# A fused four-layer kernel: 1/smooth moved from the attention outputs (DVE) to per-head copies of the values (GpSimd)

## The reference, cut to what matters

```
q, qx, k, v = fp8 linears of the normalised input     # 16 heads, 8 groups, 128 wide
kx, vx      = linear(context)                         # the "second" keys and values
core = softmax(q k^T / sqrt(128)) v                   # two heads share one k, v
xout = softmax(qx kx^T / sqrt(128)) vx
catq = fp8( clip( concat(core, xout) / proj_smooth ) )
x    = x + (catq @ wproj^T) * (proj_in_scale * proj_w_scale)
```

## Time and profile before

| | us |
|---|---|
| median of 3 runs (702.7 to 703.95) | 703.39 |
| the profiled execution | 702.4 |
| its span in the profile | 700.6 |
| PE busy | 620.0 |
| DVE busy | 552.1 |
| ACT busy | 421.5 |
| POOL busy | 275.7 |
| PEld busy | 489.9 |

### The profile page before, as it was taken

How to read it: one execution, slowest core, us unless ns; L and a number is a source line. 1 busy time by engine, 2 the same in 40 slices (tenths; PEclk the granted TensorE clock), 3 DMA queues, 4 the chain that set the end, 5 groups by cost and what they waited for, 6 DMA issues and landing times.

```text
span 700.6 us, 13484 instructions
## 1 busy us (share of the span) xinstructions
PE 620.0 (88%) x4567; PEld 489.9 (70%) x4567; DVE 552.1 (79%) x1340; ACT 421.5 (60%) x1371; POOL 275.7 (39%) x371
## 2 busy tenths in 40 slices
PE   3347989999989999999899999999999999999936
PEld 2236767766767877777687777777788778786725
DVE  7997788979676867978888578798864777769697
ACT  4247767756777746656767365668573566663531
POOL 3224574444323543434335634333332355341131
PEclk9558999999999999999999999999999999999977
DMA  9245342452583213323332222222244222110001
GB/s 274 66 181 182 136 129 69 136 160 76 156 282 114 69 75 98 99 99 98 99 114 98 99 98 99 99 98 99 99 158 98 92 106 100 17 31 1 1 0 60
DMA packets 36973, 72.87 MB, mean 104 GB/s; under 512 B 3342, under 2 KB 28586, under 8 KB 32810
## 3 DMA queue, kind: packets, MB, share of 16 engines
q1 hardware_dynamic: 36720, 72.00, 32.3%
q10 hardware_dynamic: 186, 0.02, 0.0%
HBM read 59.41 MB, written 12.60 MB: 103 GB/s over the span
## 4 chain that ended last, share of the span: by engine, by line
PE 62%; DVE 24%; issue 6%; ACT 5%; POOL 2%; DMA 1%; DVEq 0%; SPq 0%; ACTq 0%
PE bank L710 13%; PE bank L587 12%; PE bank L690 10%; PE bank L594 6%; PE bank L659 4%; PE bank L734 3%; DVE Cb L1750 3%; PE bank L676 2%; PE bank L691 2%; DVE nm L1735 2%; POOL rs L1317 2%; PE bank L820 1%; PE bank L724 1%; PE bank L829 1%; DVE Cb L1765 1%
## 5 line engine op out<-in xcount | busy, mean ns | idle before, releaser
L710 PEld LDWEIGHTS bank<-V,Pt 128*128 128x128 f32 x1024 | 126.5, 191 | 39.7 <-DVE Cb L1750 27.1
L710 PE MATMUL bank<-V,Pt 128*128 128x129 f32 x1024 | 137.9, 278 | 9.8 <-DVE Cb L1750 8.7
L1065 ACT ACTIVATE square<-bank 128x128 bf16<-128x128 f32 x372 | 98.5, 277 | 68.7 <-PE bank L587 40.9
L690 PE MATMUL bank<-QT,KTt 128*128 128x512 f32 x256 | 132.7, 600 | 2.5 <-POOL diag L1339 2.5
L1048 ACT ACTIVATE Pt<-bank 128x512 f32<-128x512 f32 x128 | 76.8, 600 | 74.2 <-PE bank L691 70.4
L1735 DVE TENSOR_REDUCE nm<-bank 128x2 f32<-128x512 f32 x128 | 82.0, 682 | 29.9 <-PE bank L676 29.7
L1317 POOL TENSOR_TENSOR rs<-ve,mhalf 128x6 f32<-128x6 f32 x64 | 94.9, 1483 | 5.3
L1339 POOL TENSOR_TENSOR diag<-identb,nm 128x512 bf16<-128x512 bf16 x64 | 67.1, 1049 | 67.0 <-DVE nm L1735 66.9
L587 PE MATMUL bank<-WQ,xq 128*128 128x256 f32 x512 | 80.3, 301 | 4.5 <-DVE xq L1636 2.7
L1750 DVE SCALAR_TENSOR_TENSOR Cb<-bank,ro,ism 128x128 bf16<-128x128 f32 x256 | 78.1, 347 | 4.5
L587 PEld LDWEIGHTS bank<-WQ,xq 128*128 128x128 f32 x512 | 68.2, 194 | 18.9 <-DVE nm L1735 12.9
(11 more groups left out here) (231 smaller groups left out, 1120.5 us busy)
## 6 DMA issues: line engine op xcount, KB each, us to landing
WQ<-wq_split SPq DMA_DIRECT2D x24, 1024.0 KB, 7.7
WH<-wh_split SPq DMA_DIRECT2D x24, 384.0 KB, 8.9
wq_split<-WQ SPq DMA_DIRECT2D x8, 1024.0 KB, 4.3
ism<-smooth_inverse SPq DMA_DIRECT2D x32, 256.0 KB, 6.4
wst<-in_L_xattn_wproj SPq DMA_DIRECT2D x16, 256.0 KB, 4.2
wh_split<-WH SPq DMA_DIRECT2D x8, 384.0 KB, 3.6
wst<-in_L_xattn_wq SPq DMA_DIRECT2D x8, 256.0 KB, 4.7
wst<-in_L_xattn_wqx SPq DMA_DIRECT2D x8, 256.0 KB, 4.4
```

The source lines that it names most:

```text
L690: nc.tensor.matmul(o[:], KTt[u % 2][:, x, t * P:(t + 1) * P], QT[u % 2][:, x, :], start=True, stop=False)
L710: last = nc.tensor.matmul(o[:, h * (P + 2):h * (P + 2) + P + 1], Pt[:, x, k, h * S + t * P:h * S + (t + 1) * P], V[u % 2][:, x, k, 0:P + 1 ...
L1065: last = A(square[:, t, h], head(t, h), ACT.Square, accum_out=ss[:, t, h:h + 1])
```

## The change

ACT now copies the values into a new tile Vr. GpSimd multiplies them by 1/smooth of each head into V, which now has a copy for each head; this is one instruction for each of the two attentions, between the second `powers` (and what the step adds) and `half`. PE weighs with the copy of the head. DVE's output is one product of both heads by 1/sum. The buffer ism is read by GpSimd, and `load_smooth` waits for its multiplies.

```
-        V = [eb(f"V{i}", [P, 2, NT, P + 4]) for i in range(2)]
+        Vr = [eb(f"Vr{i}", [P, 2, NT, P]) for i in range(2)]
+        V = [eb(f"V{i}", [P, 2, NT, HPG, P + 4]) for i in range(2)]
...
                 if u >= 2:      # load_smooth
-                    sp.wait_ge(s["o_evac"], 4 * (u - 1))
+                    sp.wait_ge(s["v_scaled"], 2 * (u - 1))
...
                 pe.wait_ge(s["exp_done"], 4 * u + 2 * x + 2)      # weigh
+                if t == 0:
+                    pe.wait_ge(s["v_scaled"], 2 * u + x + 1)
...
-                                  ..., V[u % 2][:, x, k, 0:P + 1],
+                                  ..., V[u % 2][:, x, k, h, 0:P + 1],
...
                 if u >= 2 and t == 0:      # values
-                    act.wait_ge(s["pv_done"], 4 * (u - 1))
-                A(V[u % 2][:, :, t, 0:P], QB[2 * t + 1][:]...[:, :, 1, :], ACT.Copy
+                    act.wait_ge(s["v_scaled"], 2 * (u - 1))
+                A(Vr[u % 2][:, :, t, :], QB[2 * t + 1][:]...[:, :, 1, :], ACT.Copy
                   ).then_inc(s["v_ready"], 1)
...
+            def scaled_values(u):
+                pool.wait_ge(s["v_ready"], 2 * (u + 1))
+                pool.wait_ge(s[f"ism{u % 2}_loaded"], 16 * (u // 2 + 1))
+                if u >= 2:
+                    pool.wait_ge(s["pv_done"], 4 * (u - 1))
+                for x in range(2):
+                    gp.tensor_tensor(V[u % 2][:, x, :, :, 0:P], Vr[u % 2][:, x].unsqueeze(2).to_broadcast([P, NT, HPG, P]),
+                                     ism[:, u % 2, x].rearrange("p (h d) -> p h d", h=HPG).unsqueeze(1)
+                                     .to_broadcast([P, NT, HPG, P]), ALU.mult).then_inc(s["v_scaled"], 1)
...
                 if u + 1 < UNITS:      # GpSimd's order; scaled_values(0) likewise ahead of half(0)
+                    scaled_values(u + 1)
                     half(u + 1)
...
-                if x == 0 and t == 0:      # outputs
-                    dve.wait_ge(s[f"ism{u % 2}_loaded"], 16 * (u // 2 + 1))
...
-                for h in range(HPG):
-                    last = v.scalar_tensor_tensor(out=c4[:, t, x, h, :], in0=o[:, h * (P + 2):h * (P + 2) + P],
-                                                  scalar=ro[:, x, t, h:h + 1], in1=ism[:, u % 2, x, h * P:(h + 1) * P],
-                                                  op0=ALU.mult, op1=ALU.mult)
...
+                v.tensor_tensor(c4[:, t, x], heads[:, :, 0:P], ro[:, x, t, :].unsqueeze(2).to_broadcast([P, HPG, P]), ALU.mult
+                                ).then_inc(s["o_evac"], 1)
```

More of the change, by code:

```diff
@@ L297, in build_program @@
             "xq_ready xqT_done xqT_evac ffn_done ffn_read zT_done lnT_evac y4_ready xq4_ready "
-            "qkv_done q1_done v_ready ss_ready rs_ready norm_done tr_done qt_evac hi_ready kxh_ready qxh_ready smax_done "
+            "qkv_done q1_done v_ready ss_ready rs_ready norm_done tr_done qt_evac v_scaled hi_ready kxh_ready qxh_ready smax_done "
             "max_ready diag_ready st_done exp_done pv_done o_evac cq_ready cT2_done catT_evac proj_done x3_ready "
@@ L710, in weigh @@
                         last = nc.tensor.matmul(o[:, h * (P + 2):h * (P + 2) + P + 1],
-                                                Pt[:, x, k, h * S + t * P:h * S + (t + 1) * P], V[u % 2][:, x, k, 0:P + 1],
+                                                Pt[:, x, k, h * S + t * P:h * S + (t + 1) * P], V[u % 2][:, x, k, h, 0:P + 1],
                                                 start=k == 0, stop=k == NT - 1)
@@ L1053, in values @@
                 if u >= 2 and t == 0:
-                    act.wait_ge(s["pv_done"], 4 * (u - 1))
-                A(V[u % 2][:, :, t, 0:P], QB[2 * t + 1][:].rearrange("p (x j c) -> p x j c", x=2, j=2)[:, :, 1, :], ACT.Copy
+                    act.wait_ge(s["v_scaled"], 2 * (u - 1))
+                A(Vr[u % 2][:, :, t, :], QB[2 * t + 1][:].rearrange("p (x j c) -> p x j c", x=2, j=2)[:, :, 1, :], ACT.Copy
                   ).then_inc(s["v_ready"], 1)
@@ L1261, in _ @@
             for i in range(2):
-                chain.add(gp.memset(V[i][:, :, :, P:P + 1], 1.0))
+                chain.add(gp.memset(V[i][:].rearrange("p x t h c -> p (x t h) c")[:, :, P:P + 1], 1.0))
             chain.add(gp.memset(OX[:, :, 0:1], NEG_INF))
@@ L1272, in _ @@
             chain.wait()
-            gp.memset(V[0][:, :, :, P + 1:P + 2], 1.0).then_inc(s["consts_ready"], 1)
+            gp.memset(V[0][:].rearrange("p x t h c -> p (x t h) c")[:, :, P + 1:P + 2], 1.0).then_inc(s["consts_ready"], 1)
             def norm(b, n):
@@ L1357, in _ @@
             narrow_parts(2)
+            scaled_values(0)
             half(0)
@@ L1740, in outputs @@
                 n = 4 * u + 2 * x + t
-                if x == 0 and t == 0:
-                    dve.wait_ge(s[f"ism{u % 2}_loaded"], 16 * (u // 2 + 1))
-                    if u >= 2:
-                        dve.wait_ge(s["cT2_done"], u - 1)
+                if x == 0 and t == 0 and u >= 2:
+                    dve.wait_ge(s["cT2_done"], u - 1)
                 dve.wait_ge(s["pv_done"], n + 1)
@@ L1747, in outputs @@
                 c4 = Cb[u % 2][:].rearrange("p (t x h c) -> p t x h c", t=NT, x=2, h=HPG)
-                link(v.reciprocal(ro[:, x, t, :], o[:, 0:HPG * (P + 2)].rearrange("p (h c) -> p h c", h=HPG)[:, :, P]))
-                for h in range(HPG):
-                    last = v.scalar_tensor_tensor(out=c4[:, t, x, h, :], in0=o[:, h * (P + 2):h * (P + 2) + P],
-                                                  scalar=ro[:, x, t, h:h + 1], in1=ism[:, u % 2, x, h * P:(h + 1) * P],
-                                                  op0=ALU.mult, op1=ALU.mult)
-                    if h < HPG - 1:
-                        ch.add(last)
-                last.then_inc(s["o_evac"], 1)
+                heads = o[:, 0:HPG * (P + 2)].rearrange("p (h c) -> p h c", h=HPG)
+                link(v.reciprocal(ro[:, x, t, :], heads[:, :, P]))
+                v.tensor_tensor(c4[:, t, x], heads[:, :, 0:P], ro[:, x, t, :].unsqueeze(2).to_broadcast([P, HPG, P]), ALU.mult
+                                ).then_inc(s["o_evac"], 1)
             def quantise(u):
```

## The result

The changed kernel takes 718.2 us (median of 4 runs, 717.11 to 719.28); the kernel before took 703.05 beside it. The ratio is 1.0218, with a 95% interval of 1.0200 to 1.0236: slower by 15.2 us. The forecast of 712.5 us had the direction right and the size 5.7 us too small. The profiled execution took 719.25 us with a span of 717.4.

What follows compares the result with a forecast made beforehand. TensorE was taken as the bound, fully in units without preparation, elsewhere waiting mostly for DVE. Profiled 702.4 - 4.2 + 14.0 = 712.2 us, or 713.2 on the median; 712.5 us was given, range 700.5 to 719.5.

Steps and rivals of the forecast that it cites:

- units 14, 22: the fp8 step: Multiplies take turns with DVE's two L1636; PE's wait for the output grows 2.0 us in two units, 4.0 us.
- units 0, 8, 16: the differences: Multiplies take turns with DVE's L1547 and delay the casts behind: 0.9 + 1.6 + 1.6 = 4.1 us.
- units 2, 10, 18: L1524: DVE's two-operand L1524 waits for a multiply ahead of an awaited output: 0.7 us three times, 2.1 us.
- units 26 to 28: the cast: DVE's cast starts 0.7 us later behind the second multiply, with PE full: three times, 2.1 us.
- the first unit's casts: Two DVE casts each wait for one multiply, ending about 1.3 us later; PE partly covers it: 0.8 us.
- all other units: DVE is on PSUM banks while the multiplies run, so they cost nothing there.
- The turns: DVE casts and two-operand SBUF instructions alternate with whole GpSimd multiplies: 14.0 us lost in 17 waits.
- The gain: Each DVE output 0.20 us shorter, reaching PE only at 21 waits for DVE: 4.2 us, ends 0 and 15.3.
- the moved transfer: Row of 1/smooth, wanted about a unit earlier, may delay unit 5's multiplies: 0 taken, upper end 2 us.
- Rival 1: DVE's next instruction goes ahead of waiting GpSimd ones, so DVE loses nothing: 698.2 us, at most 687.1; chance 0.14.
- rival 2: PE's busy share is mere queueing, so the full 25.6 us of DVE come through: 690.8 us; chance 0.03.
- Rival 3: GpSimd multiplies take 1.45 us instead of 1.04, losses 19.5: 717.7 us, 721.9 without gain; chance 0.10.

Runs made afterwards that it cites:

- short output: The kernel before with only the one-product output, 1/smooth left out of the result: 694.42 us, ratio 0.9875.
- filled waits: The changed kernel with 22 to 30 products into an unused bank ahead of TensorE's waits in units 1, 8, 14 and 22: 712.84 us, ratio 1.0129.
- one multiply on each side: The changed kernel with a unit's first multiply behind GpSimd's cast and the second behind the next diagonals: 701.9 us, ratio 0.9982.
- the multiplies alone: The kernel before with GpSimd's two multiplies a unit added ahead of its cast, into a tile nothing reads: 725.03 us, ratio 1.0320.
- a mix of places: The changed kernel, one multiply on each side of the diagonals, but both ahead of the cast in units 7, 12, 13, 20, 21: 697.8 us, ratio 0.9927.
- both multiplies behind the cast: The changed kernel with both multiplies behind GpSimd's cast of the second keys instead of ahead of it: 708.83 us, ratio 1.0078.
- both behind the diagonals: The changed kernel with both multiplies of a unit behind the next unit's first diagonals: 718.2 us, ratio 1.0222.
- Fills, which read nothing: The kernel before with four fills of 512 columns a unit in place of the multiplies: 709.59 us, ratio 1.0097.

## Why the forecast had the direction right and the size wrong

The delays of the last unit's cast of the keys give the sum: it ends at 628.90 us before, 622.07 with the short output alone, 637.05 with the multiplies and filled waits, 646.37 in the changed kernel. So -6.8 for the output (0.4 of it ahead of any output), +15.0 for the multiplies' blocking, +9.3 on top, against -4.2, +14.0 and nothing in the forecast. By the medians (694.42, 712.84, 718.2) the same three are -8.5, +18.4 and +5.4: the direction of each is safe, the split between blocking and what is on top only to some 4 us. The forecast came as near as 5.7 us in part by luck, since the gain that it had too small hid some of what it lacked.

| my term | forecast | filled waits against short output |
|---|---|---|
| units 14, 22: the fp8 step | 4.0 | 4.03 |
| units 0, 8, 16: the differences | 4.1 | 3.72 |
| units 2, 10, 18: L1524 | 2.1 | 1.73 |
| units 26 to 28: the cast | 2.1 | 3.06 |
| unit 1 (some 0.2 of it hidden, since the clock fell there with the short output) | 0.9 | 0.46 |
| the first unit's casts (that place shifts by itself: +1.23 in the run with one multiply on each side, which has none ahead of them) | 0.8 | 0.93 |
| all other units | 0 | 1.05 |
| sum | 14.0 | 14.98 |

- **The turns** were right as a mechanism, and the sum came near, but in part because errors cancel: unit 0 lost 0.61 where 1.6 was counted and unit 2 0.24 for 0.7, units 26 to 28 1.02 each for 0.7, and units 5, 13 and 21, put at nothing, 0.40 to 0.45 each. That only casts and two-operand instructions are stretched was too narrow: a TENSOR_SCALAR in SBUF is, too (tmp<-xs, 457 ns before, 590 after). The price of a multiply was mis-sized: 1.04 taken, 1.26 to 1.35 measured; the estimate of 1.11 from the Trainium skill (GPSIMD Engine Reference, 3.1) was nearer, and short too. It shows fully in units 26 to 28, where the second multiply ended later than counted and the cast of the keys, not of the queries, was met. Elsewhere it is offset by waits that I had counted too long.
- **The gain**, 4.2 us, was mis-sized. The step that failed is the count of 21 waits with one output each ("between two waits most chains hold one output"): 24 steps gain, eleven of them the price of two outputs or nearly so, and the weight loads wait for outputs at 36 places where the row that was counted has 10. Measured 6.4 in the delays from the first cast on, and 8.5 in the times.
- **The missing term** is TensorE's clock. I had stretched waits to 2.9 us and priced them at their own length. The changed kernel against the run with filled waits loses 6.0 us more in units 1, 8, 14 and 22 (1.2, 1.5, 1.6 and 1.7). Of the other 3.3 us, 2.0 are the clock at 0.50 ahead of the first unit, for longer than in that run: the two kernels are the same up to there, so this belongs to the execution, and why is open. Another 1.1 us come in unit 4, where the multiplies waited for the row of 1/smooth until 162.91 (issued at 157.75; a landing takes 4.7 to 8.2 us) and met unit 5's cast. That is the moved transfer, which I put at 0 of 0 to 2; in the run with filled waits they came at 160.13 and met nothing.
- **Rival 1**, DVE goes first, and **rival 2**, TensorE is not the bound, fell by the multiplies alone and by the short output alone. **Rival 3**, slow multiplies, gave a time (717.7) near the measured one by a price near the measured one, but its mechanism, all losses in proportion to the price, is not what the table shows; the runs put the difference to the clock.

## What to carry to other kernels

Before moving work from VectorE to GpSimd, lay the new instruction over VectorE's timeline and ask at each place what VectorE does then: work on PSUM banks kept its length in these runs, a cast, a TENSOR_SCALAR or a two-operand instruction in SBUF pays for up to one whole GpSimd instruction, however small it is itself. The same work cost 22 to 24 us at one place (725.03 against 702.92 with the old output, 718.2 against 694.42 with the short one) and 3.4 at a mix of places (697.8 against 694.42), and cutting the instruction in two is worth trying where the place can't be changed and DVE has one or two such instructions there, not a row of them. Where waits of TensorE grow to the 1.7 to 2.8 us seen here, what runs behind them can have a price too.

## What the runs showed that I had not expected

- In the changed kernel waits of 2.14 to 2.78 us were followed by a fall of the granted clock from 1.00 to 0.50, 1.2 to 1.7 us lost each time. The length of the wait doesn't decide it: with both multiplies behind the cast the clock fell after 1.71, 1.89 and 1.94 us; it stayed at 1.00 after 1.96 and 1.97 with both behind the diagonals, after 2.41 in unit 1 with one on each side, and after 2.60 in unit 1 of the kernel before. The Trainium skill (TensorE: Matmul & The Clock Gate, HAM oscillation) tells of the same fall to the half clock after waits on transfers; here the waits are for VectorE and GpSimd.
- 22 to 30 useless products ahead of each of four waits made the kernel faster by 5.4 us.
- Fills, which read nothing, block casts but leave two-operand instructions alone.
- Of the 6.6 us that the shorter output gave from unit 3 on, 2.7 lay in TensorE's busy time, where no wait of a matmul shows them. That they are the waits of the weight loads is likely, but not shown.
